# A language-model tower on one core: late expert loads moved to another queue and gated tile by tile, PSUM banks and step orders redone, loops written out

## The reference

```
h = take(table, x)                                    # 16 x 128 rows of 256
h = h + linear_attention(norm(h))                     # stage a: elu features, 16 heads, a cumulative sum per tile
h = h + dense(norm(h))                      # stage a: CB, SCB
h = h + performer_block(norm(h))                      # stages b and c: exp features, relu MLP 256-1024-256, norms
x = norm(h); logits = x @ router.T                    # 8 experts
e = argmax(logits); xs = x * sigmoid(max(logits))
moe = (silu(xs @ gate[e]) * (xs @ up[e])) @ down[e]   # one expert for each token
h = h + moe + (silu(x @ sg) * (x @ su)) @ sd          # a shared expert for all
```

## Time and profile before

| | us |
|---|---|
| median of 3 runs | 697.4 (695.35 to 697.88) |
| profiled execution | 697.74 |
| its span, first to last instruction | 695.9 |
| mean granted clock of TensorE | 0.978 |
| busy: TensorE / weight loads / VectorE / ScalarE / POOL | 638.5 / 518.7 / 496.9 / 288.8 / 256.4 |

### The profile page before, as it was taken

The page is one execution under the profiler, slowest core; times in us unless marked ns, Lnnn a source line. Parts: engine busy times, 40 slices in busy tenths (PEclk is TensorE's granted clock), DMA queues, the critical chain, the costliest instruction groups (busy, mean ns, idle before and its releaser), DMA issues.

```text
span 695.9 us, 15601 instructions
## 1 busy us (share of the span) xinstructions
PE 638.5 (92%) x5962; PEld 518.7 (75%) x5963; DVE 496.9 (71%) x1156; ACT 288.8 (41%) x696; POOL 256.4 (37%) x414
## 2 busy tenths in 40 slices
PE   5887799998999999999999999999938699999996
PEld 4666687886888888888888989989937365655654
DVE  3988999999999989899989988886515122223231
ACT  2345456546565454546545445553310122222121
POOL 5342335435335152332504323312200355454442
PEclk9998999999999999999999999999987899999999
DMA  7950000000000000000000000003372211011110
GB/s 262 414 223 1 9 9 10 1 17 9 9 17 2 24 2 16 2 16 15 5 16 2 16 17 3 17 16 108 26 186 67 79 40 55 28 42 61 58 52 13
DMA packets 17299, 34.22 MB, mean 49 GB/s; under 512 B 7617, under 2 KB 12240, under 8 KB 15952
## 3 DMA queue, kind: packets, MB, share of 16 engines
q1 hardware_dynamic: 11776, 18.59, 7.4%
q0 software_dynamic: 4592, 8.41, 4.1%
q10 hardware_dynamic: 864, 6.29, 3.9%
HBM read 28.74 MB, written 7.29 MB: 52 GB/s over the span
## 4 chain that ended last, share of the span: by engine, by line
PE 68%; DVE 17%; issue 6%; DMA 4%; ACT 3%; another core or an unknown queue 0%; SPq 0%; POOLq 0%; POOL 0%; DVEq 0%; ACTq 0%
PE ps L1086 63%; DMA home_rows<-send_home 3%; PE ps L1091 2%; DVE stats L710 2%; DVE S_sb L769 2%; DVE rdenTA L792 1%; PE ps L1246 1%; DVE H L726 1%; DVE rdenTB L903 1%; ACT qkA L686 1%; DVE qf L882 1%; DVE mv L711 1%; DMA yA<-x_rows,ids 1%; ACT yTB L676 1%; DVE qkA L755 1%
## 5 line engine op out<-in xcount | busy, mean ns | idle before, releaser
L1086 PE MATMUL ps<-yTC,we 128*128 128x128 f32 x1024 | 124.9, 278 | 0.0
L1086 PEld LDWEIGHTS ps<-yTC,we 128*128 128x128 f32 x1024 | 121.5, 195 | 1.2 <-issue 0.2
L368 POOL TENSOR_TENSOR var_eps<-mv,ln_eps 128x1 f32<-128x1 f32 x112 | 24.3, 217 | 256.8 <-DVE mv L711 255.0
L1086 PE MATMUL ps<-we,yTA 128*128 128x256 f32 (+1 forms) x288 | 97.9, 476 | 3.2 <-DVE S_sb L769 1.4
L1086 PEld LDWEIGHTS ps<-we,yTA 128*128 128x128 f32 x288 | 55.4, 201 | 27.5 <-issue 22.3
L1086 PE MATMUL ps<-we,yTB 128*128 128x256 f32 (+1 forms) x216 | 72.8, 468 | 0.0
L369 POOL TENSOR_TENSOR rstd<-var_eps,pow_half 128x1 f32<-128x1 f32 x112 | 65.6, 586 | 8.8
L1086 PE MATMUL ps<-we,ffT 128*128 128x256 f32 x256 | 60.8, 380 | 0.0
L1086 PEld LDWEIGHTS ps<-we,yTB 128*128 128x128 f32 x216 | 39.7, 190 | 23.4 <-issue 21.0
L1086 PEld LDWEIGHTS ps<-we,ffT 128*128 128x128 f32 x256 | 47.2, 190 | 7.4
L578 ACT ACTIVATE kf<-kf 128x1024 f32<-128x1024 f32 x16 | 16.9, 1059 | 73.4 <-DVE kf L891 73.4
(11 more groups left out here) (189 smaller groups left out, 1364.5 us busy)
## 6 DMA issues: line engine op xcount, KB each, us to landing
we<-w_experts SPq DMA_DIRECT2D x4, 1536.0 KB
we<-w_experts ACTq DMA_DIRECT2D x3, 1536.0 KB
we<-w_ff SPq DMA_DIRECT2D x2, 1024.0 KB
x_rows<-send_x SPq DMA_DIRECT2D x16, 128.0 KB, 1.7
home_rows<-send_home SPq DMA_DIRECT2D x16, 128.0 KB, 1.8
rows_sb<-rows SPq DMA_DIRECT2D x1, 1664.0 KB, 6.4
we<-w_experts ACTq DMA_DIRECT2D x3, 512.0 KB, 3.9
we<-w_qk SPq DMA_DIRECT2D x2, 512.0 KB
```

The costliest lines, as they stand in the source:

```text
L368: link(pool.tensor_tensor(var_eps[:, k:k + 1], mv[:, k, 1:2], ln_eps[:], ALU.add))
L1086: return pe.matmul(o, a, b, start=start, stop=stop)
```

## The change

- All four late experts are loaded whole by SP, from a list behind its `run_steps`: it waits until the last products that read the overlaid weights are done and until two gathered tiles were transposed (`xT_psum`), issues experts 4 and 5, the ids of group 4 (6 tiles), experts 6 and 7, the ids of group 5 (7 tiles), and then counts `experts_ready` up: once for the residents, and once more for each late expert that has landed. The stages `free_*` are gone from ScalarE's list.
- The ids come in six groups of 2, 2, 4, 2, 6 and 7 tiles.
- VectorE's `table3` makes a second table, `tile_need` = max(expert - 2, 1). In rounds 0 to 5 TensorE reads it into a register for each tile and waits for `experts_ready` to reach it ahead of the gate product; from round 6 on it waits for the constant 5.
- Ten PSUM tiles or tile groups have other banks, the waits that guard banks are changed with them, and the five lists of `run_steps` have a new order. Most of it is a turn of the old one (VectorE's lags are one less nearly throughout).
- The loops of the rounds are written out.

```diff
-    IDS_FROM = [0, MOE_SLOTS, 2 * MOE_SLOTS, 6 * MOE_SLOTS, SORTED_TILES]
+    IDS_FROM = [0, MOE_SLOTS, 2 * MOE_SLOTS, 4 * MOE_SLOTS, 5 * MOE_SLOTS, 8 * MOE_SLOTS, SORTED_TILES]
+    GROUPS = len(IDS_FROM) - 1
+    ALL_BY = 6
...
-        T2, ff0, T3, qk1, v1, dg = (ps[:, 6, :], ps[:, 2, :], ps[:, 4, :], ps[:, 4, :], ps[:, 5, :], ps[:, 6, :])
-        ctxp, ctxT, nd1, o1, T5, fa = (ps[:, 7, :], ps[:, 5, :], ps[:, 4, :], ps[:, 4, :], ps[:, 1, :], ps[:, 7, :])
-        fb, f2, T6, lo, ga, up = (ps[:, 5, :], ps[:, 6, :], ps[:, 5, :], ps[:, 2, :], ps[:, 0, :], ps[:, 1, :])
-        cn, dn, km, kb = (ps[:, 3, :], ps[:, 3, :], ps[:, 7, :], ps[:, 7, :])
-        sc = [ps[:, 5, :], ps[:, 0, :], ps[:, 1, :], ps[:, 2, :]]
+        T2, ff0, T3, qk1, v1, dg = (ps[:, 7, :], ps[:, 2, :], ps[:, 4, :], ps[:, 4, :], ps[:, 5, :], ps[:, 7, :])
+        ctxp, ctxT, nd1, o1, T5, fa = (ps[:, 7, :], ps[:, 6, :], ps[:, 4, :], ps[:, 4, :], ps[:, 0, :], ps[:, 6, :])
+        fb, f2, T6, lo, ga, up = (ps[:, 5, :], ps[:, 6, :], ps[:, 3, :], ps[:, 2, :], ps[:, 5, :], ps[:, 7, :])
+        cn, dn, km, kb = (ps[:, 1, :], ps[:, 3, :], ps[:, 7, :], ps[:, 0, :])
+        sc = [ps[:, 5, :], ps[:, 0, :], ps[:, 2, :], ps[:, 1, :]]
         qT = ps[:, 1:3, :]
-        xka = ps[:, 0:2, :]
-        xkb = ps[:, 2:4, :]
+        xka = ps[:, 2:4, :]
+        xkb = ps[:, 0:2, :]
...
-                (0, x_out), (8, ids2), (2, ids0), (5, ids1), (3, home_out), (8, ids3),
+                (1, ids0), (10, ids3), (4, ids1), (0, x_out), (8, ids2), (2, home_out),
             ])
+
+            def load_late(e):
+                sp.dma_start(we[:, e * EXPERT:(e + 1) * EXPERT], w_experts[e]).then_inc(late_loaded[e], 16)
+
+            for name, count in (("ffn0_psum", T), ("out1_psum", T), ("ff2_psum", 2 * T), ("gate_psum", T), ("up_psum", T),
+                                ("down_psum", T), ("xT_psum", MOE_SLOTS)):
+                sp.wait_ge(S[name], count)
+            load_late(RESIDENT)
+            load_late(RESIDENT + 1)
+            load_ids(4)
+            load_late(RESIDENT + 2)
+            load_late(RESIDENT + 3)
+            load_ids(5)
+            sp.wait_ge(S["residents_loaded"], 16 * RESIDENT)
+            sp.sem_inc(S["experts_ready"], 1)
+            for e in range(RESIDENT, E):
+                sp.wait_ge(late_loaded[e], 16)
+                sp.sem_inc(S["experts_ready"], 1)
...
-                (6, pA2), (5, pA), (8, r4), (7, pB), (11, scat), (7, hC), (6, r3), (9, r5), (5, r1), (8, pC), (9, r6),
-                (1, r0), (5, r2), (1, gat),
+                (2, gat), (6, pA2), (8, r4), (5, pA), (7, pB), (6, r3), (11, scat), (7, hC), (9, r5), (5, r1),
+                (1, r0), (5, r2), (8, pC), (9, r6),
...
-                (10, c_th), (2, a_rd), (5, b_cT), (4, b_yT), (8, c_tt), (1, a_par), (0, a_yT), (5, b_rqT), (4, b_x),
-                (5, b_cx2), (4, b_sq), (0, a_x), (4, b_dgc), (4, b_rk), (6, c_ra), (3, a_yT2), (13, free_dn),
-                (8, c_send), (6, c_rb), (5, free_b), (4, b_ek), (4, b_keps), (12, free_up), (7, free_ff), (0, a_exp),
-                (7, c_yT2), (11, free_ga), (4, b_eq), (5, c_yT),
+                (4, b_yT), (1, a_par), (6, c_yT), (5, b_rqT), (0, a_yT), (5, b_cx2), (4, b_x), (4, b_sq), (0, a_x),
+                (4, b_dgc), (4, b_rk), (6, c_ra), (3, a_yT2), (6, c_rb), (4, b_eq), (8, c_send), (0, a_exp),
+                (4, b_ek), (7, c_yT2), (4, b_keps), (9, c_th), (4, b_cT), (7, c_tt), (1, a_rd),
...
-                link(dve.tensor_scalar(tile_expert, sums, float(E - 1), None, ALU.min))
+                link(dve.tensor_scalar(sums, sums, float(E - 1), None, ALU.min))
+                link(dve.tensor_copy(tile_expert, sums))
+                link(dve.tensor_scalar(tile_need, sums, float(2 - RESIDENT), 1.0, ALU.add, ALU.max))
...
-                (10, c_norm), (7, b_ks), (7, b_vo), (8, b_x1), (11, c_slot), (12, table2), (13, c_hid), (6, a_ff),
-                (9, c_o), (5, a_o), (6, b_norm), (3, a_elu), (11, table0), (12, table3), (10, c_log), (9, c_res),
-                (12, c_gc), (1, a_stats), (3, a_vz), (5, a_res), (4, a_rec), (5, a_norm2), (4, a_mean), (3, a_m1),
-                (11, table1), (7, b_cx), (3, a_m2), (3, a_m3), (13, c_down), (3, a_m0), (1, a_norm), (10, c_choose),
-                (7, b_rec), (2, a_max), (7, b_mean), (6, b_dgr), (6, b_km), (6, b_qs), (6, kmx), (7, b_o),
+                (6, b_qs), (10, c_choose), (6, kmx), (7, b_o), (6, b_ks), (6, b_vo), (9, c_norm), (7, b_x1),
+                (10, c_slot), (5, a_ff), (12, table3), (12, c_hid), (10, table0), (8, c_o), (4, a_o), (5, b_norm),
+                (2, a_elu), (9, c_log), (0, a_stats), (11, c_gc), (4, a_res), (2, a_vz), (3, a_rec), (4, a_norm2),
+                (3, a_mean), (6, b_cx), (8, c_res), (10, table1), (2, a_m3), (2, a_m2), (2, a_m1), (12, c_down),
+                (2, a_m0), (10, table2), (0, a_norm), (6, b_rec), (1, a_max), (6, b_mean), (5, b_dgr), (5, b_km),
...
             def a_T0(t):
                 pe.wait_ge(S["src0_ready"], t + 1)
-                after(pe, "ff2_read", t - 6)
+                after(pe, "ctxT_ready", t - 4)
...
             def a_v(t):
                 pe.wait_ge(S["src0T_ready"], t + 1)
-                after(pe, "kexp_in", t - 3)
+                after(pe, "hT_ready", t - 9)
...
             def a_s(t):
...
-                after(pe, "gC_ready", t - 8)
...
             def a_T2(t):
...
-                if t + 3 < T:
-                    after(pe, "x_ready", (t + 3) * 4 + 4)
...
-                    after(pe, "scores_masked", (t + 2) * 4 + 3)
+                    after(pe, "scores_masked", (t + 2) * 4 + 2)
...
             def b_kmT(t):
 
                 pe.wait_ge(S["kmax_ready"], t + 1)
-                after(pe, "ffa_ready", (t - 2) * 4 + 4)
+                if t + 1 < T:
+                    after(pe, "src2T_ready", t + 2)
...
             def b_qT(t):
                 pe.wait_ge(S["qfeat_ready"], t + 1)
-                after(pe, "src5T_ready", t)
...
             def b_ctx(t):
...
+                after(pe, "ff2_read", t - 1)
...
             def b_h(t):
...
+                if t + 1 < T:
+                    after(pe, "qk1_ready", (t + 1) * 4 + 4)
...
             def c_T5(t):
                 pe.wait_ge(S["x1_ready"], t + 1)
-                after(pe, "hT_ready", t - 4)
...
             def c_fb(t):
...
+                after(pe, "gC_ready", t - 3)
...
             def c_f1(t):
...
-                if t + 3 < T:
-                    after(pe, "src2T_ready", t + 4)
...
             def c_T6(t):
...
-                if t + 3 < T:
-                    after(pe, "v1_ready", t + 4)
...
-                (8, c_lo), (6, c_T5), (2, a_num), (5, b_ctx), (2, a_den), (0, a_T0), (4, b_T3), (5, b_qT), (4, b_qk),
-                (1, a_s), (5, b_cTT), (0, a_qk), (11, c_dn), (5, b_h), (4, b_dg), (4, b_kq), (4, b_dgT), (6, c_fa),
-                (6, c_fb), (3, a_T2), (5, b_out), (4, b_kmT), (6, c_f1), (4, b_v), (4, b_kmB), (10, c_up), (8, c_cn),
-                (3, a_ffn), (6, c_f2), (2, a_out), (7, c_T6), (0, a_v), (9, c_ga),
+                (2, a_den), (4, b_T3), (0, a_T0), (5, b_qT), (4, b_qk), (5, b_cTT), (1, a_s), (11, c_dn), (0, a_qk),
+                (5, b_h), (4, b_dg), (4, b_kq), (4, b_dgT), (6, c_fa), (6, c_fb), (3, a_T2), (5, b_out), (4, b_kmT),
+                (6, c_f1), (4, b_v), (4, b_kmB), (10, c_up), (8, c_cn), (3, a_ffn), (6, c_f2), (7, c_T6), (2, a_out),
+                (9, c_ga), (0, a_v), (7, c_lo), (5, c_T5), (1, a_num), (4, b_ctx),
...
-            def expert_tiles(i, following):
-
-
-                expert = [pe.value_load(tile_expert[0:1, bass.ds(j, 1)], min_val=0, max_val=E - 1)
-                          for _, j in tiles_of(i)]
+            def expert_tiles(i):
+                expert, need = {}, {}
+                for s, j in tiles_of(i):
+                    expert[s] = pe.value_load(tile_expert[0:1, j:j + 1], min_val=0, max_val=E - 1)
+                    if i < ALL_BY:
+                        need[s] = pe.value_load(tile_need[0:1, j:j + 1], min_val=1, max_val=E - RESIDENT + 1)
                 for s, j in tiles_of(i):
                     pe.wait_ge(S["xT_ready"], j + 1)
+                    pe.wait_ge(S["experts_ready"], need[s] if i < ALL_BY else E - RESIDENT + 1)
                     for b, at, done in ((1, GATE, "eg_psum"), (2, UP, "eu_psum")):
...
-                pe.wait_ge(S["last_down_loaded"], 16)
...
-            pe.wait_ge(S["experts_loaded"], 16 * (E + 1))
-            with pe.Fori(0, ROUNDS - 2) as i:
-                expert_tiles(i, [i + 1])
-            expert_tiles(ROUNDS - 2, [ROUNDS - 1])
-            expert_tiles(ROUNDS - 1, [])
+            for i in range(ROUNDS):
+                expert_tiles(i)
```

More of the change, by code:

```diff
@@ L180, in bass_lm_tower @@
         tile_expert = sb("tile_expert", [P, SORTED_TILES], I32)[:]
+        tile_need = sb("tile_need", [P, SORTED_TILES], I32)[:]
         tile_row = sb("tile_row", [P, SORTED_TILES], I32)[:]
@@ L188, in bass_lm_tower @@
```

(27 more changed lines are left out.)

33 lines of the change are left out of this document (2 added, 31 removed).

## The result

| | before | after |
|---|---|---|
| median of 4 runs each, us | 696.8 (695.35 to 697.88) | 704.2 (703.03 to 705.18) |
| profiled execution / its span, us | 697.74 / 695.9 | 705.18 / 703.4 |
| mean granted clock | 0.978 | 0.968 |

The account below looks back on a forecast made before the run. TensorE, busy 92% of the span, was bound by its own instruction order from 290 to 460 us, with holes from 511 and 529. 697.7 + 10.0 (gate) + 1.1 (clock) + 2.5 (table) - 2.0 (pipeline) = 709.3, say 709 us; range 700 to 719.

Parts of the forecast that it names:

- The first hole goes: TensorE's 12.78 us idle at 511 to 524 us vanishes once the late loads leave the pipeline; 14.8 us won with clock.
- Rival 4: TensorE's idle at 511 us was not caused by the loads and comes again: 14.8 us more, 724 us; chance 3%.
- The gate waits for SP's whole list: First gate product waits for 21 id loads and four expert loads on SP, starting 557.0 instead of 547.0: +10.0 us.
- both holes: TensorE's pauses at 511 to 524 and 529 to 547 us: 14.8 us won before the rounds, some 25 lost at the gate.
- Rival 3: Each second load of a pair blocks SP over 4 us and round 1 comes late: 714 to 721 us; chance 13%.
- Clock: At the start of the rounds, TensorE's longer pause costs more time at half clock: +1.1 us, bounds 0 and 2.
- Second table: Two more register loads on TensorE, 0.5 us uncovered in each of rounds 1 to 5: +2.5 us, bounds 0 and 5.
- Late experts, banks: Late experts land in time, register waits of rounds 1 to 5 free; pipeline banks and order give -2 us, bounds -8, +5.
- rival 2: Moved banks remove idle time from 16 to 290 us and pay for the gate: 692 to 703 us; chance 13%.
- Rival 5: A new wait in every step slows the pipeline, over 3 us in all: 712 to 718 us; chance 9%.
- the second hole: TensorE's pause in the kernel before, read as 529 to 547 us: ids, first gathered rows and two register loads.
- rival 1: The gate costs nothing because the increments come in time; first gate product at 530, time 681 us; chance 4%.

Follow-up runs that it names:

- Experiment 4: Kernel before with only the change's PSUM banks, bank waits and step orders, ScalarE still issuing the expert loads: 694.6 us, ratio 0.995 to the kernel before.
- Experiment 9: Kernel before with ScalarE issuing the loads of experts 5 and 6 last, behind the last third of expert 7: 691.51 us, one run.
- experiment 6: Kernel before with its rounds written out on TensorE, ScalarE and VectorE, nothing else: 698.18 us, ratio 0.9986.
- experiment 7: Kernel before with TensorE's wait `last_down_loaded` moved from every round to ahead of the first, loops kept: 697.14 us, ratio 0.9981.
- experiment 1: Changed kernel with SP's `experts_ready` increment for the residents ahead of its run_steps, not behind the last id load: 683.85 us, ratio 0.9797 to the kernel before.
- experiment 2: Changed kernel with the residents' increment behind the 8 id loads of groups 1 to 3, ahead of the first late load: 685.46 us, ratio 0.9816.
- experiment 10: Kernel before with the loads of experts 5 and 6 issued by SP instead of ScalarE, at the same moment: 697.58 us, ratio 0.9992.
- experiment 3: Changed kernel with TensorE waiting for constants instead of reading the second table, increment left where it is: 701.49 us, ratio 1.0042 to the kernel before.
- experiment 5: Changed kernel with the residents' increment at SP's start and each round's register loads placed earlier, both tables kept: 677.19 us, ratio 0.9685 to the kernel before.
- experiment 8: Kernel before with expert 6's load split from expert 5's and issued with the first third of expert 7: 696.04 us, one run.

## Why the prediction was right, and where it was not

The forecast was 709 us, a loss, all of it at the gate; measured were 704.2, a loss, most of it at the gate. Step by step:

**The first hole goes: held.** Predicted for loads and clock together were 14.8 us and for the pipeline 2; the last `home_out` is issued 17.35 us earlier. Experiment 4 gives the pipeline's order 3.5 us of it (2.0 to 5.0), so the loads' share is 12 to 15, about 14. The two traces say the same: the `onehot` product would have come at 511.3 before without its wait and comes at 508.2 after, so the pipeline gave 3.1 us there, and the other 14.2 are the hole's and its half clock's. Experiment 9 shows the cause by itself, experiment 4 shows that the order isn't it. Rival 4 is out. The Trainium skill, "DMA: Bandwidth & Descriptors", section "Queues, rings and completion order", says that a DMA engine takes turns between queue rows by packets. I had kept a rival for it, since taking turns would leave a small store nearly undelayed. The store took 18.3 us beside ScalarE's pair (17.0 and 16.7 in experiments 6 and 7), 15.3 beside one load and 12.0 to 14.2 on the loads' own queue: the rule may hold packet by packet, it doesn't protect a small store here.

**The gate waits for SP's whole list: held in place and mechanism, too large in size.** From the issue of the last `home_out` to the first gate product I predicted 30.8 us, it took 26.74. Here is the mis-sized term of the sum: the four loads cost SP 0.82 + 0.91 = 1.7 us to issue, and I had taken 4.95 from the only row of SP with four such issues, which came from the start of the program and holds one issue of 3.13 us (shortest 0.43, median 0.63). The lower bound, worked out from ScalarE's quick issues, was 1.7. The 21 ids (8.20 + 5.96 + 7.51 us) and what lies between the groups took the other 25.0 us, predicted 25.8. Experiments 1 and 2 show that this list alone makes the loss. The wait is 23.59 us, and I had named 25 or more as its sign: the loads' 3.2 us are what it lacks. The net of both holes was predicted as +10.0 - 2.0 and is +3.4.

**Rival 3, SP held up by its own loads: false.** None of the four took SP over 0.43 us, though the second of ScalarE's pair had taken 4.27 us and that of experiment 10 3.55. When a second load blocks its engine stays open. It isn't the pipeline at work: the same pair beside nearly the same pipeline took 4.15 us for its second load in experiment 7 and 0.45 in experiments 4 and 6. Nor does it make the hole, which was 10.81 us in the first and 11.39 and 11.55 in the other two.

**Clock: the number was near, the reason isn't borne out.** I had +1.1 because a longer pause should cost more, and round 0 is 1.56 us longer. But experiment 6, with the waits of before, stood 0.88 us ahead of its first gate product and took 15.46 us for round 0, against 15.52 behind 23.59 us in the change. Experiment 7 took 15.20 behind 1.36 us, experiment 3 14.91 behind 24.31, experiment 1 14.55 behind 2.51, and the kernel before 13.96 behind 1.19. All of them begin the round at a granted clock of 0.50; over its second 2.5 us that is 0.88 before and 0.50 in experiment 6 and in the change. So these pauses don't order the loss, the nearness of my term is luck, and what sets the loss stays open.

**Second table: right.** +2.5 predicted; +2.1 by experiment 3. The same page of the Trainium skill, section "Latency and other measured facts", puts a `tensor_load` at some 600 ns at least. The trace has 0.30 us for each of the 12 reads (shortest, median and longest in ns):

```profile
L1346 PEldq TENSOR_LOAD <-tile_need x12: 296/302/317, 527.0 to 615.9; - x12
```

Two reads more a round, with their checks, make rounds 0.4 to 0.5 us longer than 12.23. The measured row decides. What the prediction had at nothing is the wait `last_down_loaded` that left every round. It gives 0.11 us a round back (experiment 7), which hides a part of the table's cost in rounds 1 to 5 and is all of the -0.52 in rounds 6 to 10.

**The last round: not foreseen.** +1.56 us, because the clock fell to half for the last down product. The kernels of experiments 1, 3 and 5 end at full clock, so it is no part of the change that the rounds need; I can't say why it fell in this execution.

**Late experts, banks: right.** No register wait of rounds 1 to 5 is seen, and experiment 1 shows the four loads beside rounds 0 and 1 at no cost. The idle time from 16 to 290 us went from 21.0 to 19.7 us, and rival 2 had needed 13.6 of it. Rival 5 is out too, since experiment 4 is faster than before. Two readings of mine were off and moved nothing: before, TensorE worked until 540.5 us, so the second hole began there and not at 529, and only four stages of its list have a lag one less.

**The sum.** Predicted +11.6: +8.0 for both holes, +1.1, +2.5. Measured +7.5: +3.4, +1.6, +1.5, -0.5, +1.6. Of the 4.6 us too many in the first term 3.2 are the loads' issue. On the other side stand 3.1 us of clock, in round 0 and in the last round, that no run lays to the change: in these two profiled executions the holes, the table and the wait that left make 4.4 of the 7.5 us. The medians of four differ by 7.4 us as well, and no trace shows where the other executions lost it. So 704.2 came as near to 709 as it did partly by luck. And rival 1, to which I gave 4%, was a true account of what the change could do: predicted 681, and with the increment moved 683.85.

## What to carry to other kernels

A semaphore that tells "this is ready" should be raised where it becomes true, not at the end of the issuer's list: here the residents were in place 500 us earlier, and one increment behind 21 small DMAs turned 2% won into 1% lost. When transfers are moved onto a queue engine, add up all its instructions between the last thing that the next stage needs and the signal that it waits for; at 1.0 to 1.15 us an id load they are the price, not the bytes. Put register loads behind a batch of products, not ahead of it.

## What the runs showed of the hardware beyond that

- A 128 KB store that lands in 1.7 us earlier in the pipeline, and in 1.7 to 5.8 us at this place in the change, without loads beside it, took 12 to 19 us beside one or two loads of 1.5 MB, from whichever of the two queues these came (before, experiments 8 and 10).
- The second of two loads issued back to back held its engine for 4.27 us, 4.15 (experiment 7) and 3.55 us (experiment 10, SP's pair of 4.03) beside the pipeline, but for 0.45 us in the same place in experiments 4 and 6, and for no more than 0.43 us in the change and in experiment 1, beside the rounds. What decides it isn't shown.
- A met semaphore wait on TensorE costs 0.11 us where the next products are waited for, and nothing that shows where the queue of products is full (experiments 7 and 3).
